# Moving layer 1 of the first token chunk directly behind its layer 0 in a four-layer attention kernel

## What is computed

```
x = x + L0_xattn(layernorm(x), ctx)      # softmax attention, 16 heads of 16
x = x + L0_ffn(layernorm(x))             # ternary weights, 1024 hidden, low-rank term
x = x + L1_xattn(layernorm(x), ctx)
x = x + L1_ffn(layernorm(x))             # gated MLP, plus 4 x 8 experts per token out of a table:
                                         #   de = down_embed[indices]; ue = up_embed[indices]
                                         #   ew = silu(sum(h * de)) * softmax(scores); sum(ew * ue)
x = x + L2_xattn(layernorm(x), ctx)      # keys and queries rotated by position
x = x + L2_ffn(layernorm(x))             # 8 experts, top 2, plus a shared one
x = x + L3_xattn(layernorm(x), ctx)      # autocorrelation attention
x = x + L3_ffn(layernorm(x))             # 8 experts, top 2
```

## Time and profile before

| | us |
|---|---|
| median of 3 runs | 1779.86 (1776.69 to 1780.30) |
| the profiled execution | 1789.62 |
| its span on the core | 1787.8 |
| PE busy in the span | 1384.3 (77%) |
| VectorE busy | 1121.7 (63%) |
| ScalarE busy | 810.9 (45%) |
| GpSimd busy | 689.3 (39%) |

### The profile page before, as it was taken

One profiled execution on the slowest core, in us unless ns is written; L12 is line 12 of the kernel. 1 busy time (PEld: TensorE's weight loads), 2 busy tenths in 40 slices (PEclk: granted clock), 3 DMA queues, 4 the chain that ended last, 5 costly groups with the idle time before them and its releaser, 6 DMA issues.

```text
span 1787.8 us, 19004 instructions
## 1 busy us (share of the span) xinstructions
PE 1384.3 (77%) x5858; PEld 687.2 (38%) x5858; DVE 1121.7 (63%) x3025; ACT 810.9 (45%) x2050; POOL 689.3 (39%) x705
## 2 busy tenths in 40 slices
PE   5888888766759786666657676777888997886998
PEld 3344444332335434332323432433443443532444
DVE  6431414478876967998887987888443344426265
ACT  2344353445837686645646647747443330210010
POOL 1000000058847788876866688886000010010000
PEclk7689898977969788787678788988999998998999
DMA  5000000045535657665656656664000021011000
GB/s 209 21 1 1 9 7 0 1 127 157 166 107 157 179 161 205 175 167 134 183 142 186 156 168 179 181 172 122 23 16 0 28 85 31 1 44 44 4 12 24
DMA packets 59382, 169.08 MB, mean 95 GB/s; under 512 B 15632, under 2 KB 20304, under 8 KB 58640
## 3 DMA queue, kind: packets, MB, share of 16 engines
q0 software_dynamic: 40960, 134.25, 27.4%
q1 hardware_dynamic: 18320, 33.61, 6.0%
HBM read 163.00 MB, written 4.82 MB: 94 GB/s over the span
## 4 chain that ended last, share of the span: by engine, by line
PE 44%; DVE 18%; POOL 14%; issue 9%; ACT 7%; DMA 5%; SPq 1%; another core or an unknown queue 1%; DVEq 0%; POOLq 0%; ACTq 0%
POOL bufR L1821 12%; PE psum L1148 5%; PE psum L1014 4%; PE psum L821 3%; PE psum L944 3%; PE psum L980 2%; PE psum L1092 2%; DVE bufB L1508 2%; PE psum L1026 2%; PE psum L845 2%; PE psum L870 2%; PE psum L952 2%; ACT bufR L1247 2%; PE psum L873 2%; PE psum L1071 2%
## 5 line engine op out<-in xcount | busy, mean ns | idle before, releaser
L1821 POOL DMA_INDIRECT bufR<-in_table,rowid x512 | 550.7, 1076 | 284.4 <-issue 126.3
L1173 ACT ACTIVATE bufR<-bufR 128x256 f32<-128x256 f32 x512 | 205.5, 404 | 76.6 <-DVE bufR L1380 44.3
L821 PE MATMUL psum<-bufB 32*128 32x308 f32 x768 | 145.2, 573 | 84.2 <-DVE bufB L1508 61.9
L1508 DVE TENSOR_REDUCE bufB<-psum 128x4 f32<-128x616 f32 x192 | 147.7, 794 | 93.8 <-PE psum L821 91.0
L1380 DVE TENSOR_TENSOR bufR<-bufR 128x1024 f32<-128x1024 f32 x128 | 160.2, 1252 | 48.3 <-DMA bufR<-in_table,rowid 46.5
L1014 PE MATMUL psum<-xtf,wf 128*128 128x512 f32 x320 | 158.1, 640 | 35.6 <-DVE x_sb L1669 15.2
L1848 POOL TENSOR_TENSOR x_sb<-x_sb,wattn 128x256 f32<-128x256 f32 x16 | 11.0, 724 | 309.4 <-DMA wattn<-in_attn 187.5
L821 PEld LDWEIGHTS psum<-bufB 32*128 32x128 f32 x768 | 58.9, 222 | 169.5 <-DVE bufB L1508 98.8
L1841 POOL TENSOR_TENSOR x_sb<-x_sb,wattn 128x256 f32<-128x256 f32 x32 | 24.3, 790 | 246.1 <-DMA wattn<-in_attn 192.4
L1182 ACT ACTIVATE bufR<-bufR,ew 128x256 f32<-128x256 f32 x128 | 63.9, 503 | 117.2 <-DVE ew L1388 79.0
L980 PE MATMUL psum<-xtf,wf 128*128 128x512 f32 x128 | 82.2, 801 | 44.4 <-DVE bufR L1575 23.9
(11 more groups left out here) (237 smaller groups left out, 2532.3 us busy)
## 6 DMA issues: line engine op xcount, KB each, us to landing
bufR<-in_table,rowid POOLq DMA_INDIRECT x512
wf<-in_ffn SPq DMA_DIRECT2D x2, 2304.0 KB, 18.6
bufR<-in_ffn SPq DMA_DIRECT2D x1, 2696.5 KB, 15.9
wattn<-in_attn SPq DMA_DIRECT2D x4, 641.0 KB
wf<-in_rope SPq DMA_DIRECT2D x4, 512.0 KB
bufB<-in_ffn SPq DMA_DIRECT2D x1, 2048.0 KB, 8.4
scr_corr<-bufR SPq DMA_DIRECT2D x16, 128.0 KB, 2.4
bufR<-scr_corr SPq DMA_DIRECT2D x4, 512.0 KB
```

Source lines behind the costliest of these rows:

```text
L821: ins = mm(psum[:, 2 * (u % 2) + z, 0:PAR * S], q[r, g, i * P:(i + 1) * P], keysm[r, g, b, :, 0:S], start=True, stop=True)
L1173: own.mark(act(row, row, ACT.Identity, accum_out=dots[:, g % 4, j:j + 1]))
L1508: eng.reduce_max(m4[:, i, :].rearrange("p (z r) -> p z r", z=BANDS)[:, 2 * side:2 * side + 2, PAR * g:PAR * g + PAR], psum[:, at:at + 2, 0 ...
L1821: eng.indirect_dma_start(ring[:, s * GRP + j, :], None, io["table"], bass.IndirectOffsetOnAxis(ap=rowid[c % 2][:, at + j:at + j + 1], axis ...
```

## The change

The sequence becomes A00, A10, A01, A02, A11, A03, A12, A13, A20, A21, A22, A23. `next_queries` holds the layernorm and queries of the next attention; where that attention's input isn't there yet (A10 right behind A00 needs F00), they now stand behind the feed-forward part instead of ahead of it. `KV_ORDER` gives the sequence of keys and values: layer 0 and layer 1 of batch 0, then of batch 1, then layer 2. The two places go by layer instead of by batch for layers 0 and 1 (`KV_PLACE`), `KV_LEFT` names the attention that last used a place, and keys of layer 2 are computed behind the feed-forward part. Since layers alternate more often, the weights are loaded more often: keys' five times after the first load instead of three, queries' and output's seven times instead of five.

```diff
-A_ORDER = ((0, 0), (0, 1), (1, 0), (1, 1), (0, 2), (0, 3), (1, 2), (1, 3), (2, 0), (2, 1), (2, 2), (2, 3))
+A_ORDER = ((0, 0), (1, 0), (0, 1), (0, 2), (1, 1), (0, 3), (1, 2), (1, 3), (2, 0), (2, 1), (2, 2), (2, 3))
...
-KV_AFTER = {1: (1, 0), 5: (1, 1), 7: (2, 0), 9: (2, 1)}
+
+KV_ORDER = ((0, 0), (1, 0), (0, 1), (1, 1), (2, 0), (2, 1))
+KV_PLACE = {(0, 0): 0, (1, 0): 1, (0, 1): 0, (1, 1): 1, (2, 0): 0, (2, 1): 1}
+KV_LEFT = {(0, 1): (0, 1), (1, 1): (1, 1), (2, 0): (0, 3), (2, 1): (1, 3)}
+KV_AFTER = {POS[0, 1]: (0, 1), POS[1, 1]: (1, 1), POS[0, 3]: (2, 0), POS[2, 1]: (2, 1)}
...
+def next_queries(k):
...
     for k, (layer, c) in enumerate(A_ORDER):
         a_out = attention(layer, c, k, kv_in[layer, c // 2], q_in)
-        if k in KV_AFTER:
-            kl, kb = KV_AFTER[k]
-            kv_in[kl, kb] = kv(kl, kb)
-            if kb:
-                load("kv", kl + 1, 5.0, kv_in[kl, kb])
+        layer2 = k in KV_AFTER and KV_AFTER[k][0] == 2
+        if k in KV_AFTER and not layer2:
+            kv_in[KV_AFTER[k]] = kv(*KV_AFTER[k])
...
+        early = more and A_ORDER[k + 1] in x_ready
+        if early:
+            q_in = next_queries(k + 1)
...
+        if layer2:
+            kv_in[KV_AFTER[k]] = kv(*KV_AFTER[k])
+        if more and not early:
+            q_in = next_queries(k + 1)
...
             def first_pass(layer, c, u):
-                k, b = chunk(layer, c), c // 2
+                k, b = chunk(layer, c), KV_PLACE[layer, c // 2]
...
                 if what == "kv":
-                    eng.wait_ge(kv_v, B * n)
-                    eng.wait_ge(kv_vc, B * n)
-                    weights(n, ("wk", "bv"), ld_kv)
+                    eng.wait_ge(kv_v, KV_RUNS[n - 1][-1] + 1)
+                    eng.wait_ge(kv_vc, KV_RUNS[n - 1][-1] + 1)
+                    weights(KV_PIECES[n], ("wk", "bv"), ld_kv)
```

More of the change, by code:

```diff
@@ L130, in kv @@
         banks[0] = parts[0] = k3
+        if KV_ORDER.index(item) == KV_RUNS[n][-1]:
+            load("kv", n + 1, 5.0, k3)
         return k3
@@ L302, in plan @@
     q_in = queries(0, 0, xt, 0)
-    kv_in[0, 1] = kv(0, 1)
-    load("kv", 1, 5.0, ("DVE", ("kv", 0, 1)))
+    if RUNS[0][-1] == 0:
+        load("q", 1, 5.0, q_in)
+    kv_in[1, 0] = kv(1, 0)
     for r in range(4):
@@ L318, in plan @@
     prev, x_ready = (), {(0, c): ("SP", ("in", "x")) for c in range(NCH)}
+    def next_queries(k):
+        layer, c = A_ORDER[k]
+        done = queries(layer, c, front("a", layer, c, x_ready[layer, c]), k)
+        n = PIECE_AT[k]
+        if k == RUNS[n][-1]:
+            load("q", n + 1, 5.0, done)
+        if layer == 2 and c < NCH - 1:
+            load("rope", c + 1, 6.0, ("DVE", ("Q", 2, c)))
+        return done
     for k, (layer, c) in enumerate(A_ORDER):
         a_out = attention(layer, c, k, kv_in[layer, c // 2], q_in)
-        if k in KV_AFTER:
-            kl, kb = KV_AFTER[k]
-            kv_in[kl, kb] = kv(kl, kb)
-            if kb:
-                load("kv", kl + 1, 5.0, kv_in[kl, kb])
+        layer2 = k in KV_AFTER and KV_AFTER[k][0] == 2
+        if k in KV_AFTER and not layer2:
+            kv_in[KV_AFTER[k]] = kv(*KV_AFTER[k])
         n = PIECE_AT[k]
@@ L328, in plan @@
             load("o", n + 1, 5.0, ("PE", ("y", layer, c, TI - 1)))
-        if k + 1 < len(A_ORDER):
-            nl, n_c = A_ORDER[k + 1]
-            xt = front("a", nl, n_c, x_ready[nl, n_c])
-            q_in = queries(nl, n_c, xt, k + 1)
-            n = PIECE_AT[k + 1]
-            if k + 1 == RUNS[n][-1]:
-                load("q", n + 1, 5.0, q_in)
-            if nl == 2 and n_c < NCH - 1:
-                load("rope", n_c + 1, 6.0, ("DVE", ("Q", 2, n_c)))
-        if k == len(A_ORDER) - 1:
+        more = k + 1 < len(A_ORDER)
+        early = more and A_ORDER[k + 1] in x_ready
+        if early:
+            q_in = next_queries(k + 1)
+        if not more:
             keys0, values_in = kv3()
@@ L1030, in keys3 @@
             def keys3():
[L1031 removed]
+                eng.wait_ge(ld_kv, 16 * len(KV_PIECES))
                 shared_banks(("K3",))
```

49 lines of the change are left out of this document (27 added, 22 removed).

## The result

The changed kernel takes 1845.89 us (median of 4 runs, 1839.55 to 1852.89), the kernel before 1780.08 (4 runs): a ratio of 1.0372, interval 1.0323 to 1.0421. It is 66 us slower. The forecast was 24 us slower; the sign was right, the size was not, and the time lies above the range.

A forecast was written before the change was run, and what follows sets the result against it. The rings of fetches, not PE, were taken to bound the middle stage, with chunk 2's row numbers decisive. 1789.6 + 21 (those numbers later) + 3 (late keys) = 1813.6 us profiled, 1804 against the median; range 1768 to 1832.

The forecast's parts named there:

- A01 beside F10: Attention A01 with feed-forward part F10: 94 us, as A11 beside F10 before, with chunk 0's row numbers 88.5 us in.
- the 300 us: From chunk 0's row numbers at 320.5 us to chunk 1's at 620.5, 88.5 us behind A11's end at 532.
- the rest: From chunk 2's row numbers to the end: 974.8 us, order unchanged but for one detail, plus 3 us for late keys.
- The open step: At the start, feed-forward part F00 and attention A10 run apart: 129 us, where A01 beside F00 cost 92.
- The row numbers of chunk 0: Ready at 320.5 us, 49 us earlier than the 369.57 of before, so the first ring starts earlier.
- The hole: GpSimd idles some 90 us between fetching chunk 0 and chunk 1; part of the slower forecast, chance 0.54.
- Chunk 1 to chunk 2: From chunk 1's row numbers at 620.5 us to chunk 2's at 834: a ring of 213.5 us.
- The clock: If F00's own 30 us at the start ran at the slow clock, A10 would end up to 25 us later.
- 15 us off A13's step: Up to chunk 2's row numbers, A13 beside F12 takes 102.6 us, not 117.6, as queries and layer 2's keys leave.
- signs of being wrong: A10 ending well before 220 us, GpSimd's gap under 40 us, or the rest behind chunk 2's numbers over 10 us shorter.
- The head start survives: Rival: cheaper early steps bring chunk 2's row numbers at 798 us, 15 us earlier; 1768 us in all; chance 0.24.
- Much slower: Rival: 25 us for the clock and 10 for layer 2's keys on top, up to 1840 us; chance 0.10.

The follow-up runs named there:

- after_third: The changed kernel unaltered, run again on chip D: 1820.2 us, ratio 1.0287 to the kernel before.
- before_again: The kernel before, unaltered, run again on chip D for its trace: 1772.25 us, ratio 1.0012.
- kv2_early_2: The changed kernel with layer 2's keys of both batches back at the places of before, on chip D: 1809.13 us, ratio 1.0221.
- after_again: The changed kernel unaltered, run again on chip C: 1847.84 us, ratio 1.0323 to the kernel before.
- kv2_early: The changed kernel with layer 2's keys of both batches back at the places of before, on chip A: 1808.87 us, ratio 1.0193.
- a02_kv2_early: The changed kernel with sequence A00, A01, A10, A02, A11, A03, A12 and layer 2's keys at the places of before, on chip C: 1804.06 us, ratio 1.0054.
- both_undone: The changed kernel with before's order of attentions and before's places for layer 2's keys, on chip D: 1772.8 us, ratio 1.0032.

## Why the prediction was wrong in size

The sum of the prediction ended at 1813.6 us for a profiled execution; 1850.6 was measured, 37.0 more. The other 5 us are offset: the trace of before stood 9.8 us above its median, that of after 4.7. The mechanism that was forecast came. What failed are three terms of its sum: A01 beside F10 was priced at 94 us and took 105.8; the 300 us from chunk 0's row numbers to chunk 1's were 315.3; and the rest behind chunk 2's row numbers, taken as unchanged but for 3 us, grew by 17. The 37 us, term by term:

| term | forecast | measured | off |
|---|---|---|---|
| start to A10's end | 232 | 227.9 | -4.1 |
| from there to row numbers of chunk 0 | 88.5 | 100.4 | +11.9 |
| to row numbers of chunk 1 | 300 | 315.3 | +15.3 |
| to row numbers of chunk 2 | 213.5 | 213.7 | +0.2 |
| to the end of the span | 977.8 | 991.6 | +13.8 |

On chip D, where waits without a releaser are rare, after_third's row numbers of chunk 2 stand 28.4 us later than before_again's, forecast 21, and its rest is 17.9 us longer, forecast 3. So without such waits the rest is the term that misses most, and the 300 us hold.

**What held.** The open step: 129 forecast, 129.2 measured, and not by luck of two errors: A10's first pass starts 61.9 us behind A00's end (forecast 62.6) and A10 takes 67.3 from there (66). A00 itself ended 4.4 us earlier, the steps for chunk 1 that I had taken at nothing. The row numbers of chunk 0: 320.5 forecast, 328.22 measured. The hole: some 90 forecast from fetch to fetch, 106.3 measured, of which GpSimd idled 86.38 in one wait. The step of A03 with F11: 94 forecast, 98.2. Chunk 1 to chunk 2: 213.5 forecast, 213.7. The mechanism of the forecast, a head start lost to a step without overlap with a hole in GpSimd's work behind it, is what the traces show. "The clock" as a rival, 25 us in the open step, did not come: its condition was that F00 runs slow as well, and F00 ran at 0.97; the low clock, 0.64, fell on A10, where the price of the scores held it already.

**First miss: A01 beside F10 at 94 us.** I took A11 beside F10 for it, and overlooked that keys of layer 0 for batch 1 are made in this step now. VectorE can store them only when A01 is done with the place that they take. PE's timeline of after, in order of time: keys (3.4 us in three rows, the first shown), two pieces of F10 behind waits for VectorE, two more, and transposes that wait for VectorE to release the banks of the keys.

```profile
250.97 1.31 PE L818 MATMUL psum<-ctxt,wattn 128*128 128x154 f32 x8
...
259.12 5.40 PE L1000 MATMUL psum<-xtf,wf 128*128 128x512 f32 x8 [3.32 <-DVE bufR L1596]
...
272.11 5.40 PE L1000 MATMUL psum<-xtf,wf 128*128 128x512 f32 x8 [3.10 <-DVE bufR L1596]
...
286.92 5.40 PE L1000 MATMUL psum<-xtf,wf 128*128 128x512 f32 x8
...
299.75 3.70 PE L1000 MATMUL psum<-xtf,wf 128*128 128x512 f32 x8
...
325.63 1.94 PE L798 MATMUL psum<-const,xa 128*128 128x128 f32 x8 [3.56 <-DVE bufB L1518]
```

In the kernel before, the same four pieces (L980) beside A11:

```profile
306.77 3.70 PE L980 MATMUL psum<-xtf,wf 128*128 128x512 f32 x8
...
318.06 5.40 PE L980 MATMUL psum<-xtf,wf 128*128 128x512 f32 x8 [3.10 <-DVE bufR L1575]
...
333.65 4.57 PE L980 MATMUL psum<-xtf,wf 128*128 128x512 f32 x8
...
345.65 3.70 PE L980 MATMUL psum<-xtf,wf 128*128 128x512 f32 x8
```

Worked out: 3.4 us of keys, 3.6 of the wait for their banks, 3.3 for a second wait on VectorE, and 2.5 for the four pieces (19.9 us against 17.4; the granted clock of the step is 0.85, and was 0.92). Together 12.8, of which the step shows 11.8. In after_third the step costs 105.6 us, and 105.8 or 105.9 in after_again, kv2_early and kv2_early_2, so it is the kernel's. My sentence "keys of layer 1 come in; I take nothing for them" was right for layer 1 and had no counterpart for layer 0.

**Second miss: from chunk 0 to chunk 1, 300 us.** In after_third it was 302.1, near the forecast, but by two errors that cancel: A11 ends 208.0 us behind chunk 0's row numbers (forecast 211.5), and chunk 1's stand 94.0 behind A11's end (forecast 88.5). The result has 220.6 and 94.8. Its trace has some 10 us in two stretches in which VectorE stood idle and PE too, with no releaser in the records. Timeline of VectorE:

```profile
349.34 0.80 DVE L1529 TENSOR_REDUCE bufB<-psum 128x4 f32<-128x616 f32 x1 [5.41 <-remote]
354.93 0.80 DVE L1529 TENSOR_REDUCE bufB<-psum 128x4 f32<-128x616 f32 x1 [4.79 <-remote]
```

and of PE:

```profile
350.20 1.40 PE L841 MATMUL psum<-bufB 32*128 32x308 f32 x4 [5.68 <-issue]
```

The step of A02 took 103.1 us with them and 93.2 without, in after_third; on chip C, where such waits are many, it took 107.5. No step of mine had a term for that.

**Third miss: "the rest".** I measured from the row numbers of chunk 2 to the end and held that distance at 974.8 us, as "the order is the same before and after except for one detail", plus 3 us. It was 962.9 in before_again, 964.2 in kv2_early_2 and 980.7 in after_third. A13's end parts it in two:

| | before_again | kv2_early_2 | after_third |
|---|---|---|---|
| row numbers of chunk 2 to A13's end | 36.1 | 38.8 | 45.7 |
| A13's end to the end of the span | 926.7 | 925.4 | 935.0 |

I took 15 us off A13's step ahead of the row numbers, for queries and keys that leave it. On chip D 20.0 went (100.5 us against 120.5 from A12's end), but the whole step became only 10.3 us shorter (146.2 against 156.5), so about half of the gain returns between the row numbers and A13's end. A20's queries are one piece that crosses: PE runs them at 741.5 us in before_again, ahead of the row numbers at 809.17, and at 878.1 in after_third, behind those at 837.56. The other half lies behind A13's end and is absent in kv2_early_2, so it goes with the late keys; against that kernel A20's step makes 7.9 us of it. I had costed these by PE's wait at A22 alone (4.47 us), in the wrong step: A22's step takes 142.6 us with the keys early and late. None of my signs of being wrong asked for a longer rest.

**The rivals.** "The head start survives" did not happen: the 61 us won up to the end of chunk 0's fetches are gone at the first fetch of chunk 1. It had the Trainium skill beside it ("Perfetto Trace Analysis", section Optimization Strategy), which says that interleaving regimes with different most-contended engines may improve performance. The case agrees in a detail and not in the result: F11 without a ring beside it is cheap, 98.2 us against 119 for A02 with F11, but the regime that starts early leaves the other without a partner, for 129 us against 92.

"Much slower" had the late keys of layer 2 at 10 us, and 12 were measured. It looked for them in the wrong place, a wait of over 5 us at A13's transposes; PE didn't wait there:

```profile
742.36 1.09 PE L798 MATMUL psum<-const,xa 128*128 128x128 f32 x8
```

And its 25 us for the clock in the open step did not come. I had treated the late keys as an alternative to the hole, with a chance of 0.10 and outside the range. They were an addition to it, and nearly all the small misses fell on the same side.

## What to carry to other kernels

Before a dependent step is pulled ahead, count the steps left that have an independent partner: the step that loses its partner costs its full length, and a head start elsewhere pays for it only if the later chain can use it; here 61 us of head start met 101 of gap. When the cost of a change is measured from a moment to the end, check that the chain behind the moment moves with it: here the row numbers came 7.3 us earlier by the late keys, and the attention beside them ended when it had before. List the work that crosses the moment, and add it where it arrives. A price taken from a similar step holds only if the step carries the same small guests; the keys of another batch were 12 us in a step of 94.

## What was not expected of the hardware

The same kernels differ between chips in a kind of idleness for which the records name no releaser. Summed over PE, VectorE and ScalarE, idle time marked issue or remote is 205 us in the trace of before and 168 in that of after; on chip C 179 to 234 in four kernels; on chips A and D 10 to 14 in eight. Apart from the 10 to 14 us that the quiet traces have too, those of before, after and chip C all lie between the first fetch of chunk 0 and A22's end, so they appear only in the part of the kernel where rings run. The largest entries of after, engine by engine:

```profile
PE psum L841 <- issue: 26.6, 11, 5.7
...
DVE bufB L1529 <- remote: 15.5, 3, 5.4
...
ACT bufR L1193 <- issue: 20.2, 9, 10.8
```

The kernel before has a span of 1787.8 us with them and 1772.0 without, the changed one 1848.8 and 1818.3. So the gap between the two is 61 us with these waits and 46 without, and the ratios are 1.0372 and 1.0287. The kernel before is also slower where there are many: 1780 and 1795 us (the result, chip C) against 1775 and 1769 (A and D). Chip B doesn't fit well: 1783 us, with 36 and 75 us of such waits in its two traces, which are of kernels with half the fetches. What the waits are stays open, since nothing that the kernels changed switched them, and so does why the changed kernel loses more by them. That neither key of layer 2 alone moved the time on chip C, while both together did on chip D, may be for the same reason or within the spread of chip C's runs; it was not settled.

No version that does all the work is faster than the kernel before; a02_kv2_early and both_undone come nearest, at 1.0054 and 1.0032.
